# The scan's first two chunks started inside the projection's last steps, and the product of u with its sigmoid on VectorE

## The chip, the cores and the metric

The kernel runs on one NeuronCore of a Trainium2 chip. The metric is the time of one execution on the device in microseconds (us), as a median of several runs. The engines are named as in the profile: PE is TensorE's matmul, PEld its weight load, DVE is VectorE, ACT is ScalarE, POOL is GpSimd, and SP is the engine whose queue issues the DMAs. An engine executes its own program in order, and engines wait for one another on semaphores.

## The reference

Two layers over 8 images of 192 channels and 64x64 positions (L = 4096 positions), all in float32. Only the first layer is touched:

```python
xn = layernorm over channels of x
xz = einsum('dc,bchw->bdhw', in_proj_w, xn);  xc, z = split(xz, 2)
xc = silu(conv3x3_depthwise(xc) + conv_b)             # silu(u) = u * sigmoid(u)
xs = [xc, xc transposed, both reversed]               # 4 directions k
x_dbl = einsum('kcd,bkdl->bkcl', x_proj_w, xs);  dts, Bv, Cv = split(x_dbl, [12, 16])
dt = softplus(dt_proj_w @ dts + dt_proj_b)
h_t = exp(dt_t * A) * h_(t-1) + dt_t * B_t * u_t;  y_t = sum over n of h_t * C_t      # 4 states n
y = layernorm(sum of the 4 directions + Ds * xs) * silu(z);  x = x + out_proj_w @ y
```

The second layer is a non-local attention over the 4096 positions of each image (softmax of theta^T phi, then a weighted sum of g and a projection).

## The kernel before

One loop runs over the 8 images. In an image four stages follow one another: the projection (`run_project`), the scan (`run_chunks`), the mix (`run_mix`) and the attention (`run_attend`). Between two stages stands `barrier`: each engine drains, increments `stage_done`, and waits until all five have done so. No barrier stands inside a stage; there every engine has its own program of the same steps, ordered by hand, and semaphores with running counts link them.

**The projection** works on 8 chunks of 512 positions (`NCH` = 8, `T` = 512). `step(c, par, which)` does parts of four different chunks at once: with "n" it normalizes chunk c+1 (mean and variance by PE, `da`, `db`, `na`, `nb` on DVE), with "p" it projects chunk c (PE, L360 and L361) and makes `gate` = z * sigmoid(z), with "c" it convolves chunk c-2, and with "u" it finishes chunk c-3. The convolution of the first 128 channels is eight multiply-adds on DVE (L1039); that of the other 64 is six matmuls on PE (`remainder`, L371), which ACT takes from bank 5 into `u` (L694, semaphore `rem_free`). ACT then makes the sigmoid of u in the buffer `cs` by Exp, Ln and Exp (L681, L683, L685), and POOL multiplies `u` by `cs` in place (L937, semaphore `u_ready`). There is one buffer `cs`, so that the sigmoid of chunk w waits for the product of chunk w-1. Steps 3 to 6 are a loop that holds "npcu"; step 7 is "pcu", steps 8 and 9 are "cu", and step 10 is "u".

**The scan** walks 32 chunks (4 directions of 8). Counting from the scan's start as g, a chunk takes this path: PE's `xdbl` (L409, L410) projects u; ACT copies the result to `xd` (L729, `copy_xd`) and to `xhl` (L735, `copy_high`), and DVE takes the rest (`low_half`, L1084); SP saves rows of `xd` to memory and loads them back, broadcast to all partitions, into `bs` (L297 to L303); PE's `dtproj` (L417) makes the input of the softplus; ACT does five instructions on it (`soft_abs` to `soft_log`, L739 to L755), POOL adds one part to `dt` (`residue`, L945), DVE the other (`residue`, L1090, and `softplus`, L1096); POOL makes `du` = dt * u (`times_u`, L951) and `dbu` = B * du in three pieces (`drive`, L960); ACT makes the decays (L762), DVE scans (L1106) and multiplies by C (L1114), which PE spreads (`spread`, L428) and sums. DVE works on one chunk while the others prepare the next one or two. Ahead of the first chunk's scans stands a written-out head that prepares chunks 0 and 1.

The buffers of the scan (`xd`, `xhl`, `dt`, `bs`, `dbu`, `h` and others) lie over those of the projection (`xa`, `xb`, `na`, `nb`, `zs`, `cs` and others). Line numbers here and in the prediction are those of the kernel before.

## Time and profile before

| what | value |
|---|---|
| median of 3 runs | 9796.43 us (9791.25 to 9798.18) |
| the profiled execution, its own time | 9790.28 us |
| its span, first to last instruction | 9788.5 us |
| mean granted clock of PE over the span | 0.966 |
| busy: PE, DVE, ACT, POOL | 93%, 76%, 64%, 35% |
| chain of work that ended last: PE, issue, DVE, ACT, POOL | 68%, 13%, 13%, 3%, 2% |

An image takes about 1,220 us and all eight look alike. The profile has a page, with sums over the whole span, and views: busy time of the engines in chosen stretches, groups by line, and a timeline. In the timeline a row gives the start, the duration of the run of equal instructions, the engine and line, what is written from what, the count (x2), and in brackets how long the engine had been idle before it and who ended that. A float32 matmul of 512 columns shows as two records.

### The profile page before, as it was taken

Reading aid. Unit: us, or ns where it says so; the run is one execution under the profiler, and the core shown is the slowest. Engines: PE = TensorE matmul, PEld = TensorE weight load, DVE = VectorE, ACT = ScalarE, POOL = GpSimd, SP = SyncE. Lnnn points to the kernel's source line nnn. Section 1 sums busy time; section 2 is a strip of 40 time slices with the busy share of each in tenths; the row PEclk is TensorE's granted clock in tenths of the full one; section 3 lists DMA queues with packets and bytes.
Section 4 is the critical chain, followed back from the end, with each engine's and each line's share of the span. In section 5 each row is a group of like instructions: output and inputs, shape, how many; then the busy total and the mean of one; then the engine's idle time right before and its main releaser. Section 6 shows DMA issues by size and latency. Waiting matters only on the chain.

```text
span 9788.5 us, 105912 instructions
## 1 busy us (share of the span) xinstructions
PE 9055.4 (93%) x27076; PEld 4819.9 (49%) x27076; DVE 7434.1 (76%) x8241; ACT 6228.0 (64%) x7692; POOL 3449.1 (35%) x1937
## 2 busy tenths in 40 slices
PE   7999989999799998999979999899998999989999
PEld 3336733367333673336733367333663336633366
DVE  6987769876698766987669776697766977679776
ACT  5765667656676566765667556676566755667555
POOL 3850038500385003850038500485004850048500
PEclk9999989999899998999999999899999999989999
DMA  1320013200132001320013200132001320013200
GB/s 56 106 75 12 11 52 105 74 13 12 51 109 71 12 12 51 110 70 11 12 56 106 70 11 12 57 108 67 10 12 57 111 65 10 13 56 110 65 10 13
DMA packets 214540, 499.71 MB, mean 51 GB/s; under 512 B 71001, under 2 KB 71993, under 8 KB 181262
## 3 DMA queue, kind: packets, MB, share of 16 engines
q1 hardware_dynamic: 214030, 494.10, 16.5%
q8 instruction: 174, 2.85, 0.1%
q14 instruction: 336, 2.75, 0.1%
HBM read 466.39 MB, written 27.38 MB: 50 GB/s over the span
## 4 chain that ended last, share of the span: by engine, by line
PE 68%; issue 13%; DVE 13%; ACT 3%; POOL 2%; DVEq 1%; SPq 0%; ACTq 0%; POOLq 0%; DMA 0%
DVE h L1106 7%; PE ps L587 5%; PE ps L574 5%; PE ps L589 5%; PE ps L588 5%; PE ps L575 5%; PE ps L576 5%; PE ps L494 4%; PE ps L417 3%; PE ps L455 3%; PE ps L353 2%; PE ps L452 2%; PE ps L409 2%; PE ps L354 2%; PE ps L436 2%
## 5 line engine op out<-in xcount | busy, mean ns | idle before, releaser
L1232 DVE TENSOR_TENSOR pl<-pf,ph 128x1024 fp32r<-128x1024 f32 x1024 | 1254.4, 1225 | 1017.1 <-ACT ph L886 1008.9
L1106 DVE TENSOR_TENSOR_SCAN h<-ps,h,dbu 128x512 f32<-128x512 f32 x1536 | 1884.5, 1268 | 17.3 <-DVE h L1132 5.3
L960 POOL TENSOR_TENSOR dbu<-bs,du 128x1024 f32<-128x1024 f32 x768 | 1799.1, 2373 | 52.8 <-POOL du L951 52.8
L886 ACT ACTIVATE ph<-pf 128x1024 fp32r<-128x1024 f32 x1024 | 1085.7, 1060 | 762.8 <-PE ps L589 762.6
L906 POOL MEMSET sqb<- 64x512 f32 x16 | 8.3, 519 | 4002.3 <-issue 3997.4
L880 ACT ACTIVATE pf<-ps 128x1024 f32<-128x1024 f32 x1024 | 1050.0, 1025 | 531.4 <-PE ps L576 531.4
L762 ACT ACTIVATE ps<-dt,negA 128x512 f32<-128x512 f32 x1536 | 1033.3, 684 | 443.7 <-DVE h L1106 408.9
L1216 DVE TENSOR_REDUCE mx<-ps 128x1 f32<-128x512 f32 x1792 | 1168.6, 683 | 78.2 <-PE ps L494 59.6
L1114 DVE TENSOR_TENSOR hc<-h,ps 128x1024 f32<-128x1024 f32 x768 | 937.9, 1221 | 190.6 <-PE ps L428 107.3
L951 POOL TENSOR_TENSOR du<-dt,u 128x512 f32<-128x512 f32 x512 | 706.5, 1402 | 625.8 <-DVE dt L1096 625.8
L574 PE MATMUL ps<-thc,phh 97*128 97x512 f32 x2048 | 845.0, 413 | 6.7 <-ACT thc L863 6.7
L587 PE MATMUL ps<-ph,gth 128*97 128x512 f32 x2048 | 819.0, 400 | 11.7 <-DVE pl L1232 8.7
L575 PE MATMUL ps<-thc,phl 97*128 97x512 f32 x2048 | 814.2, 398 | 0.0
L576 PE MATMUL ps<-thc,phh 97*128 97x512 f32 x2048 | 811.7, 396 | 0.0
L589 PE MATMUL ps<-pl,gth 128*97 128x512 f32 x2048 | 810.2, 396 | 0.0
L428 PE MATMUL ps<-xhl,selr 128*128 128x512 f32 x1536 | 692.5, 532 | 126.6 <-DVE hc L1114 126.5
L588 PE MATMUL ps<-ph,gtl 128*97 128x512 f32 x2048 | 808.9, 395 | 0.0
L494 PE MATMUL ps<-phh,thc 96*128 96x512 f32 x1824 | 633.7, 408 | 47.3 <-POOLq L180 18.8
L945 POOL TENSOR_TENSOR dt<-dt,ze 128x1024 f32<-128x1024 f32 x256 | 605.4, 2365 | 101.5 <-ACT dt L755 101.5
L417 PE MATMUL ps<-xd,wdt 128*128 128x512 f32 x1024 | 520.2, 632 | 101.9 <-DVE dt L1096 94.8
L428 PEld LDWEIGHTS ps<-xhl,selr 128*128 128x128 f32 x1536 | 265.4, 190 | 589.9 <-DVE hc L1114 379.8
L1039 DVE SCALAR_TENSOR_TENSOR u<-pad,vecs,u 128x512 f32<-128x512 f32 (+1 forms) x512 | 491.0, 960 | 61.4 <-DVE db L1027 18.8
(188 smaller groups left out, 15586.0 us busy)
## 6 DMA issues: line engine op xcount, KB each, us to landing
bs<-rows SPq DMA_DIRECT2D x256, 1024.0 KB, 5.1
bs<-rows SPq DMA_DIRECT2D x512, 256.0 KB, 6.1
xa<-in_x SPq DMA_DIRECT2D x130, 256.0 KB, 2.9
xb<-in_x SPq DMA_DIRECT2D x130, 128.0 KB, 3.0
out<-fa SPq DMA_DIRECT2D x64, 256.0 KB, 2.0
rdb<-rden SPq DMA_DIRECT2D x56, 192.0 KB, 3.4
out<-fa SPq DMA_DIRECT2D x64, 128.0 KB, 2.3
rows<-xd SPq DMA_DIRECT2D x256, 8.0 KB
```

Of the source, the lines that this page charges most:

```text
L574: mm(dst, kk, thc[par][0][:, :], start=True, stop=False)
L575: mm(dst, phl[:, m * P:(m + 1) * P], thc[par][0][:, :], start=False, stop=False)
L576: q = mm(dst, kk, thc[par][1][:, :], start=False, stop=True)
L587: mm(dst, gth[:, m, :], ph[:, mp % 2, e, :], start=(m == 0), stop=False)
L588: mm(dst, gtl[:, m, :], ph[:, mp % 2, e, :], start=False, stop=False)
L589: q = mm(dst, gth[:, m, :], pl[:, mp % 2, e, :], start=False, stop=(m == MT - 1))
L880: A(pf[:, mp % 2, :, :], ps[:, 2 * (mp % 2):2 * (mp % 2) + 2, :], ACT.Exp)\
L886: A(ph[:, mp % 2, :, :], pf[:, mp % 2, :, :], ACT.Copy).then_inc(S["ph_ready"], 1)
L960: pool.tensor_tensor(dbu[:, q, :, :], bs[par][:, q, :, :], du[:, r:r + 1, :].to_broadcast([P, 2, T]), ALU.mult).then_inc(S["dbu_ready"], 1)
L1106: dve.tensor_tensor_scan(h[:, j, ::step], ps[:, 2 + e, ::step], dbu[:, q, e, ::step], h[:, j, end:end + 1], ALU.mult, ALU.add)\
L1216: dve.tensor_reduce(mx[:, t, m:m + 1], ps[:, 5 + j % 2, :], AX.X, ALU.max)\
L1232: TT(pl[:, mp % 2, :, :], pf[:, mp % 2, :, :], ph[:, mp % 2, :, :].bitcast(F32), ALU.subtract)\
```

## The change

The barrier between the projection and the scan is removed, and the remaining three are renumbered. Of the head of the scan, pieces are moved between the projection's steps 8, 9 and 10, by a function `early(n)` that `run_project` calls ahead of step 8 + n. What the barrier guarded is guarded by waits on single semaphores. The product of `u` with `cs` goes from POOL to DVE, at the end of a step. The clearing of `xd` and `xhl` on DVE goes to the image's start, and that of `h` stays ahead of the first scan.

```diff
         def run_project(eng, step, early=None):
             ...
             step(NCH - 1, 1, "pcu")
-            step(NCH, 0, "cu")
-            step(NCH + 1, 1, "cu")
-            step(NCH + 2, 0, "u")
+            for n, which in ((0, "cu"), (1, "cu"), (2, "u")):
+                if early:
+                    early(n)
+                step(NCH + n, n % 2, which)
# SP
-                barrier(sp, b, 0)
+                sp.wait_ge(S["xc_ready"], b * NCH + NCH)
+                sp.sem_inc(mark, 1)
# PE
-                xdbl(0, 0, g_0)
-                dtproj(0, g_0)
+                def early(n):
+                    if n == 0:
+                        pe.wait_ge(S["u_ready"], b * NCH + 2)
+                        pe.sem_inc(mark, 1)
+                        xdbl(0, 0, g_0)
+                        dtproj(0, g_0)
+                    elif n == 1:
+                        pe.wait_ge(S["u_ready"], b * NCH + 3)
+                        pe.sem_inc(mark, 1)
+                        xdbl(0, 1, g_0 + 1)
+                run_project(pe, step, early)
+                dtproj(0, g_0 + 1)
+                pe.wait_ge(S["gate_ready"], b * NCH + (NCH + 1))
+                pe.wait_ge(S["rem_free"], b * NCH + (NCH + 1))
+                pe.sem_inc(mark, 1)
                 spread(0, 0, g_0)
-                xdbl(0, 1, g_0 + 1)
-                dtproj(0, g_0 + 1)
+                pe.wait_ge(S["u_ready"], b * NCH + (NCH + 1))
                 run_chunks(pe, b, body)
# ACT
-                copy_xd(g_0)
-                copy_high(0, g_0)
-                soft_abs(g_0)
-                soft_relu(g_0)
-                soft_exp(g_0)
-                soft_one(g_0)
-                soft_log(0, g_0)
-                copy_xd(g_0 + 1)
+                def early(n):
+                    if n == 0:
+                        act.wait_ge(S["scan_set"], b + 1)
+                        copy_xd(g_0)
+                        copy_high(0, g_0)
+                    elif n == 1:
+                        soft_abs(g_0)
+                        soft_relu(g_0)
+                        soft_exp(g_0)
+                        soft_one(g_0)
+                        soft_log(0, g_0)
+                    else:
+                        copy_xd(g_0 + 1)
+                        copy_high(1, g_0 + 1)
+                run_project(act, step, early)
+                act.wait_ge(S["gate_ready"], b * NCH + (NCH + 1))
+                act.sem_inc(mark, 1)
                 decay(0, 0, 0, g_0 * NP, 0, g_0)
                 decay(0, 0, 1, g_0 * NP, 0, g_0)
                 soft_abs(g_0 + 1)
                 soft_relu(g_0 + 1)
                 soft_exp(g_0 + 1)
-                copy_high(1, g_0 + 1)
                 soft_one(g_0 + 1)
                 soft_log(1, g_0 + 1)
# POOL
-                def step(c, par, which):
-                    if "u" in which:
-                        ...
-                        pool.tensor_tensor(u[:, :, sl], u[:, :, sl], cs[:, :, :], ALU.mult).then_inc(S["u_ready"], 1)
                 residue(0, g_0)
+                pool.wait_ge(S["u_ready"], b * NCH + 2)
                 times_u(0, 0, 0, g_0)
-                for q in range(NP):
-                    drive(q, g_0 * NP + q, 0, g_0)
+                pool.wait_ge(S["xc_ready"], b * NCH + NCH)
+                pool.sem_inc(mark, 1)
+                drive(0, g_0 * NP, 0, g_0)
+                drive(1, g_0 * NP + 1, 0, g_0)
+                residue(1, g_0 + 1)
+                drive(2, g_0 * NP + 2, 0, g_0)
+                pool.wait_ge(S["u_ready"], b * NCH + (NCH + 1))
# DVE, end of step(c, par, which)
+                    if "u" in which:
+                        w = b * NCH + (c - 3)
+                        dve.wait_ge(S["cs_ready"], w * 3 + 3)
+                        sl = bass.ds((c - 3) * T, T)
+                        TT(u[:, :, sl], u[:, :, sl], cs[:, :, :], ALU.mult).then_inc(S["u_ready"], 1)
# DVE, body of the scan: the second residue goes behind the first scans
                         if q == 0 and nxt:
-
+                            if not before:
+                                residue(g + 1)
                             softplus(1 - par, g + 1)
# DVE, head of the scan
-                low_half(0, g_0)
-                residue(g_0)
-                softplus(0, g_0)
-                low_half(1, g_0 + 1)
-                residue(g_0 + 1)
+                def early(n):
+                    if n == 1:
+                        low_half(0, g_0)
+                    elif n == 2:
+                        residue(g_0)
+                        softplus(0, g_0)
+                        low_half(1, g_0 + 1)
+                run_project(dve, step, early)
+                dve.wait_ge(S["u_ready"], b * NCH + (NCH + 1))
+                dve.wait_ge(S["rem_ready"], b * NCH + NCH)
+                dve.sem_inc(mark, 1)
+                dve.memset(h[:, :, T - 1:T], 0.0).then_inc(S["zero_h"], 1)
+                dve.wait_ge(S["zero_h"], b * (K + 3) + 4)
+                dve.sem_inc(mark, 1)
```

The order of DVE's instructions around the border of the two stages. Before, the last multiply-add of chunk 7 is followed by the barrier (L181), three clearings, and the whole head of the scan:

```order
L1039 SCALAR_TENSOR_TENSOR u<-pad,vecs,u 128x512
L181 ISA
L1075 MEMSET xd 128x512
L1076 MEMSET h 128x6
L1078 MEMSET xhl 64x512 x2
L1079 ISA
L1083 ISA
L1084 TENSOR_TENSOR xhl<-ps,xhl 32x512
L1089 ISA
L1090 SCALAR_TENSOR_TENSOR ps<-ps,za 128x1024
L1096 SCALAR_TENSOR_TENSOR dt<-ps,dt 128x1024
L1083 REGISTER_ALU
```

In the changed kernel (its own line numbers: L1052 is the multiply-add, L1087 the product with `cs`, L1096 `low_half`, L1102 `residue`, L1108 `softplus`) the same place on DVE reads:

```order
L1052 SCALAR_TENSOR_TENSOR u<-pad,vecs,u 128x512
L1085 ISA
L1087 TENSOR_TENSOR u<-u,cs 128x2x512
L1101 ISA
L1102 SCALAR_TENSOR_TENSOR ps<-ps,za 128x1024
L1108 SCALAR_TENSOR_TENSOR dt<-ps,dt 128x1024
L1095 REGISTER_ALU
L1096 TENSOR_TENSOR xhl<-ps,xhl 32x512
L1087 TENSOR_TENSOR u<-u,cs 128x2x512
L1161 MEMSET h 128x6
```

The first L1087 is the product of chunk 6, the second that of chunk 7; the softplus of chunk 0 and `low_half` of chunk 1 now stand between them. The same border on ACT, before: the last two chunks' copies and sigmoids (L694 to L685), the barrier (L181), then the first copy of the scan:

```order
L694 ACTIVATE u<-ps,vecs 128x512
L700 REGISTER_ALU
L681 ACTIVATE cs<-u 128x1024
L683 ACTIVATE cs<-cs 128x1024
L685 ACTIVATE cs<-cs 128x1024
L181 ISA
L723 REGISTER_ALU
L726 ISA
L728 ISA
L729 ACTIVATE xd<-ps 20x512
```

In the changed kernel ACT has, from the softplus of chunk 0 on (L745 to L761), the copy and sigmoid of chunk 6 (L706, L693 to L697) and the copies of the scan's chunk 1 (L735, L741):

```order
L756 ACTIVATE ps<-za 128x1024
L760 REGISTER_ALU
L761 ACTIVATE dt<-za 128x1024
L706 ACTIVATE u<-ps,vecs 128x512
L693 ACTIVATE cs<-u 128x1024
L694 ISA
L695 ACTIVATE cs<-cs 128x1024
L696 REGISTER_ALU
L697 ACTIVATE cs<-cs 128x1024
L734 ISA
L735 ACTIVATE xd<-ps 20x512
L740 ISA
```

The five softplus instructions of chunk 0 stand ahead of the sigmoid of chunk 6, and `copy_xd` of chunk 1 stands ahead of that of chunk 7.

## Rows read from the trace of the kernel before

**Rows 1.** Busy time by stretch; after POOL the granted clock, DMA share and GB/s

```profile
105.35:119.08 13.73, 13.73 (x33) 6.06 (x32) 11.49 (x15) 11.47 (x16) 2.63 (x1) 1.00 0.00 0
133.90:166.10 32.20, 21.34 (x48) 8.85 (x49) 25.13 (x27) 20.43 (x23) 10.22 (x4) 0.91 0.00 0
166.10:192.50 26.40, 14.81 (x20) 5.63 (x21) 6.53 (x9) 12.97 (x16) 11.39 (x6) 0.63 0.38 121
207.70:222.50 14.80, 13.04 (x31) 5.28 (x30) 13.94 (x13) 11.60 (x17) 11.33 (x6) 1.00 0.34 107
```

**Rows 2.** Timeline of TensorE (PE) in the projection's loop: start, duration, line, count

```profile
119.08 1.02 PE L353 MATMUL ps<-xa,avg 128*128 128x512 f32 x2
...
127.67 5.31 PE L371 MATMUL ps<-pad,tapw 128*128 x12
```

**Rows 3.** Timeline of VectorE (DVE) in the projection's loop

```profile
121.00 0.69 DVE L1026 TENSOR_TENSOR da<-xa,ps 128x512 f32<-128x512 f32 x1 [0.60 <-PE ps L354]
...
122.73 2.54 DVE L1039 SCALAR_TENSOR_TENSOR u<-pad,vecs,u  x3 [0.45 <-DVE db L1027]
...
127.24 4.41 DVE L1039 SCALAR_TENSOR_TENSOR u<-pad,vecs,u  x3 [0.16 <-DVE u L1039]
131.57 0.68 DVE L1063 TENSOR_TENSOR na<-da,rstd 128x512 f32<-128x512 f32 x1
...
133.37 0.67 DVE L1068 TENSOR_TENSOR gate<-ps,zs 64x512 f32 x1
```

**Rows 4.** The convolution's line on VectorE: minimum, median, maximum in ns

```profile
L1039 DVE SCALAR_TENSOR_TENSOR u<-pad,vecs,u x512: 733/752/2743, 65.5 to 8699.6; - x86, 128x512 f32<-128x512 f32 x85
```

**Rows 5.** The page's group of a VectorE product with both inputs in SBUF

```profile
L1232 DVE TENSOR_TENSOR pl<-pf,ph 128x1024 fp32r<-128x1024 f32 x1024 | 1254.4, 1225 | 1017.1 <-ACT ph L886 1008.9
```

**Rows 6.** Timeline of all engines, the projection's last steps

```profile
139.35 5.31 PE L371 MATMUL ps<-pad,tapw 128*128 128x512 f32 x12
...
142.75 0.78 ACT L717 ACTIVATE u<-ps,vecs 128x512 f32<-128x512 f32 x1
...
144.70 0.69 ACT L694 ACTIVATE u<-ps,vecs 128x512 f32<-128x512 f32 x1 [1.17 <-PE ps L371]
145.47 1.06 ACT L681 ACTIVATE cs<-u 128x1024 f32<-128x1024 f32 x1
...
163.41 2.34 POOL L937 TENSOR_TENSOR u<-u,cs 128x1024 f32<-128x1024 f32 x1 [5.60 <-ACT cs L685]
```

**Rows 7.** Timeline of all engines, the scan's head

```profile
166.10 2.07 PE L409 MATMUL ps<-u,wx 128*128 128x512 f32 x2 [8.92 <-POOLq L180]
...
166.78 1.03 DVE L1078 MEMSET xhl<- 64x512 f32 x2 [0.17 <-issue]
...
170.00 0.59 ACT L729 ACTIVATE xd<-ps 20x512 f32<-20x512 f32 x1 [6.66 <-PE ps L410]
...
174.36 1.02 ACT L739 ACTIVATE za<-ps 128x1024 f32<-128x1024 f32 x1 [3.30 <-PE ps L417]
...
179.35 2.34 POOL L945 TENSOR_TENSOR dt<-dt,ze 128x1024 f32<-128x1024 f32 x1 [13.60 <-ACT dt L755]
...
181.80 1.23 DVE L1096 SCALAR_TENSOR_TENSOR dt<-ps,dt 128x1024 f32<-128x1024 f32 x1 [2.23 <-POOL dt L945]
...
183.19 2.49 POOL L951 TENSOR_TENSOR du<-dt,u 128x512 f32<-128x512 f32 x2 [1.51 <-DVE dt L1096]
...
185.93 6.96 POOL L960 TENSOR_TENSOR dbu<-bs,du 128x1024 f32<-128x1024 f32 x3 [0.25 <-POOL du L951]
```

**Rows 8.** Timeline of VectorE, the scans of the first two chunks

```profile
192.52 2.46 DVE L1106 TENSOR_TENSOR_SCAN h<-ps,h,dbu 128x512 f32<-128x512 f32 x2
...
207.72 2.46 DVE L1106 TENSOR_TENSOR_SCAN h<-ps,h,dbu 128x512 f32<-128x512 f32 x2
```

**Rows 9.** Busy time and granted clock of a stretch without matmuls

```profile
160.00:162.00 2.00, 0.00 (x0) 0.00 (x0) 0.00 (x0) 1.86 (x2) 0.00 (x0) 0.61 0.00 0
```

**Rows 10.** The page's DMA issues: the line of the broadcast loads

```profile
bs<-rows SPq DMA_DIRECT2D x512, 256.0 KB, 6.1
```

More of the change, by code:

```diff
@@ L174, in build @@
         mark = sem("mark")
-        stages = 4
+        stages = 3
         def barrier(eng, b, n):
@@ L225, in run_chunks, with run_project @@
                     body(k, n % 2, b * G + (k * NCH + n), place(k, n - 1), place(k, n), place(k, n + 1), place(k, n + 2))
-        def run_project(eng, step):
+        def run_project(eng, step, early=None):
             step(-1, 1, "n")
@@ L304, in _ @@
                 run_chunks(sp, b, body)
-                barrier(sp, b, 1)
+                barrier(sp, b, 0)
                 with sp.Fori(0, NCH // 2) as cc:
@@ L308, in _ @@
                         load(b, (b * 2 + 1) * NCH + cc * 2 + q, cc * 2 + q, q)
-                barrier(sp, b, 2)
+                barrier(sp, b, 1)
                 for q in range(2):
@@ L337, in _ @@
                 store(NCH - 1)
-                barrier(sp, b, 3)
+                barrier(sp, b, 2)
             sp.wait_ge(S["out_stored"], nb * (32 * NCH) + 32)
@@ L400, in step @@
                         remainder(c - 2)
-                run_project(pe, step)
-                barrier(pe, b, 0)
                 def xdbl(k, c, g):
@@ L546, in _ @@
                 run_mix(pe, step)
-                barrier(pe, b, 2)
+                barrier(pe, b, 1)
                 def theta(c, i, before):
@@ L650, in _ @@
                 output(last, 1)
-                barrier(pe, b, 3)
+                barrier(pe, b, 2)
         @block.scalar
@@ L718, in step @@
                           scale=vecs[:, V_TAP + 4:V_TAP + 5]).then_inc(S["tap_ready"], 1)
-                run_project(act, step)
-                barrier(act, b, 0)
-                act.wait_ge(S["scan_set"], b + 1)
                 def copy_xd(g):
@@ L813, in _ @@
                 add_y1(K - 1, 0, g_0 + G - 1)
-                barrier(act, b, 1)
+                barrier(act, b, 0)
                 def split_theta(i, par):
@@ L855, in _ @@
                 run_mix(act, step)
-                barrier(act, b, 2)
+                barrier(act, b, 1)
                 def take_shift(i, par):
@@ L890, in _ @@
                 read_sum(i_0 + (NCH - 1))
-                barrier(act, b, 3)
+                barrier(act, b, 2)
         @block.gpsimd
@@ L929, in _ @@
                                                None, ALU.mult).then_inc(S["tapw_ready"], 1)
-                def step(c, par, which):
-                    if "u" in which:
-                        w = b * NCH + (c - 3)
-                        pool.wait_ge(S["cs_ready"], w * 3 + 3)
-                        sl = bass.ds((c - 3) * T, T)
-                        pool.tensor_tensor(u[:, :, sl], u[:, :, sl], cs[:, :, :], ALU.mult).then_inc(S["u_ready"], 1)
-                run_project(pool, step)
-                barrier(pool, b, 0)
                 def residue(par, g):
@@ L964, in body @@
                     if nxt:
-                        residue(1 - par, g + 1)
+                        if before:
+                            residue(1 - par, g + 1)
                         times_u(*nxt, 1 - par, g + 1)
@@ L986, in _ @@
                     pool.sem_inc(mark, 1)
+                barrier(pool, b, 1)
                 barrier(pool, b, 2)
-                barrier(pool, b, 3)
         @block.vector
@@ L1069, in step @@
                             .then_inc(S["gate_ready"], 1)
-                run_project(dve, step)
-                barrier(dve, b, 0)
+                    if "u" in which:
[3 more added lines that the diff above has]
+                        TT(u[:, :, sl], u[:, :, sl], cs[:, :, :], ALU.mult).then_inc(S["u_ready"], 1)
                 dve.memset(xd[:, :], 1.0).then_inc(S["zero_h"], 1)
-                dve.memset(h[:, :, T - 1:T], 0.0).then_inc(S["zero_h"], 1)
                 for t in xhl:
                     dve.memset(t[R:P, :].bitcast(F32), 0.0).then_inc(S["zero_h"], 1)
-                dve.wait_ge(S["zero_h"], b * (K + 3) + 4)
+                dve.wait_ge(S["zero_h"], b * (K + 3) + 3)
                 dve.sem_inc(S["scan_set"], 1)
@@ L1209, in _ @@
                 run_mix(dve, step)
-                barrier(dve, b, 2)
+                barrier(dve, b, 1)
                 def top(j, i):
@@ L1296, in _ @@
                 finish(NCH - 1, last, 1)
-                barrier(dve, b, 3)
+                barrier(dve, b, 2)
 def kernel(x, L0_conv_ln_w, L0_conv_ln_b, L0_conv_in_proj_w, L0_conv_conv_w, L0_conv_conv_b, L0_conv_x_proj_w,
```

6 lines of the change are left out of this document (3 added, 3 removed).

## The prediction, made before the changed kernel ran

> **What bounds the kernel now.** I read the stages first. In the projection's loop the busy view shows one step of 13.73 us in which PE is busy for all of it, at the full clock, and DVE for 11.49 [rows 1]. The timeline agrees: the mean of the next chunk starts 13.73 us after the last one, and the step ends with twelve records of `remainder` (5.31 us) [rows 2]. In the scan DVE is the bound: busy 13.94 of 14.80 us, PE 13.04 [rows 1]. Between these two lies the border that the change touches: from the loop's end (133.9) to the barrier PE is busy for 21.34 of 32.20 us, and in the next 26.40 us, the scan's head, DVE for 6.53, ACT for 12.97 and PE for 14.81, at a mean clock of 0.63 [rows 1]. There no engine is the bound. It is a chain of single steps, and that is what a reader should see in the rows of the head: nearly each has some microseconds of idle time in its bracket [rows 7]. The border costs as much in each of the eight images.
>
> The figure to follow is the start of the scans of the scan's chunk 1, at 207.72, since from there on DVE works in its steady rhythm; chunk 0's begin at 192.52 [rows 8].
>
> **The product on DVE, in the loop.** It adds eight instructions per image. The same shape with both inputs in SBUF takes 1.225 us on DVE while POOL is idle [rows 5]. It also takes POOL's product away, and that gives DVE something back. The convolution's instruction takes 0.752 us in the median, but up to 2.743 [rows 4], and the run of three at 127.24 took 4.41 us against 2.54 for the run at 122.73 [rows 3]: 1.87 us more, in the stretch in which POOL's product ran. So DVE's sum per step is -1.87 + 1.22 = -0.65 us. The Trainium skill ("SBUF — State Buffer", who interferes with whom) gives the mechanism: a VectorE instruction with two SBUF inputs and a GpSimd instruction that reads SBUF exclude each other, the later one waiting for the whole of the earlier. By that rule the trace agrees.
>
> Is the loop faster for it? The product stands behind `gate` and ahead of the next `da`. Without the stretch the convolution ends at 129.7 in place of 131.57; `na` then waits for ACT's `rstd` until about 130.95, so that `gate` ends at 133.4 in place of 134.04 [rows 3] and the product at 134.65. The next `da` is due at 121.00 + 13.73 = 134.73, when PE's mean is ready (its row had waited 0.60 us for PE). It is not late. Nor is it earlier, because PE has no idle time. I cost the loop at nothing; the cover is PE, and without it a step would take DVE's own 12.4 us, a gain of 1.3. The clearings (two of `xhl` 1.03 us [rows 7], that of `xd` about half as much) go to the image's start, ahead of DVE's first work, which waits there for PE's first mean. I cost them at nothing too, or 1.5 us per image if that cover is gone.
>
> **The border, step by step.** I use the first image's clock. The waits that come last decide each line.
>
> 1. ACT ends step 7 at 143.6, as now (142.75 + 0.78) [rows 6]. PE ends `remainder` of chunk 5 some 0.6 us sooner than 139.35 + 5.31 = 144.66, because `gate` is sooner: 144.0.
> 2. New: PE does `xdbl` of the scan's chunk 0 (four records at 0.43 us, the full-clock rate of rows 2, to 145.8), and ACT, in order, waits for it, then does two copies (0.6 and 0.5), to 147.0. Behind that wait ACT's copy of chunk 5 and its sigmoid are queued, 0.7 + 3.2 us (L694 to the end of L685; three at 1.06 [rows 6]): 150.9, where it was 148.7. PE does `dtproj` to 148.4 and `remainder` of chunk 6 to 153.7.
> 3. ACT's five softplus instructions, from 174.36 until POOL takes over at 179.35 [rows 7], 4.9 us,, end at 155.8; copy and sigmoid of chunk 6 at 159.6; two copies at 160.7. PE ends `xdbl` of chunk 1 at 155.5, and `remainder` of chunk 7, which waits for ACT's copy, at 161.7.
> 4. ACT's copy and sigmoid of chunk 7: 165.8, now 163.34. So u is complete 2 us later than now (165.75, the end of POOL's last product [rows 6]). That is the price of interleaving.
> 5. DVE: product 5 at 152.1, `low_half` 0.7, convolution of chunk 7 to 159.1; POOL's `residue` of chunk 0 falls in it, from 155.8, which costs the 1.87 us: 160.9. Product 6 to 162.15, `residue` and `softplus` of chunk 0 at 1.23 each: 164.5. That softplus ends now at 181.80 + 1.23 = 183.03 [rows 7]: 18.5 us later.
> 6. POOL: `du` 2.5 us (183.19 [rows 7]) to 167.1; then its first `drive` (6.96 / 3 = 2.3 us) and DVE's product 7 want the same stretch, and the first scan starts at about 170.2 where it is 192.52: between 169.6, if they don't meet, and 170.8.
> 7. Chunk 0: scans and product with C 3.7 us (173.9), then on DVE the moved `residue` 1.2, and `softplus` of chunk 1, which waits for POOL's `residue`, itself behind two `drive`s: 176.7. ACT's five for chunk 1 end at 172, in time. Then 2 x 3.7 + 0.7 + 1.2 us: 186.1.
>
> Against 207.72 that is 21.6 us. SP's DMAs are moved too: rows of chunk 0 are saved from 146.5 on and loaded back 6.1 us after issue [rows 10], long before `drive` at 167; those of chunk 1 from 160 on, for a `drive` at 180; SP has nothing else queued.
>
> From this I take two deductions. PE's clock reads 0.61 in the stretch 160 to 162, after PE's last matmul at 166.10 - 8.92 = 157.2 [rows 7, 9]. In my schedule PE has no such pause until 170, when it waits 3.8 us for the first hc; `dtproj` of chunk 2 might then run at half clock, 3.7 for 1.7 us, and make the last `spread` and product of chunk 0 up to 1.5 us late. Half of it: 0.6. And some 20 handovers that I counted too short: 0.5. That makes **20.5 us per image, 164 us for eight**. The sum is made against the profiled execution's own 9790.28 us (span 9788.5 and 1.8 around it): 9626. The median of the runs lies 6.15 us above the profiled one, so that I predict **9632 us**.
>
> The likeliest case's own range: a sum of single steps that misses by 3 to 4 us per image, 9605 to 9665.
>
> **The rivals.**
>
> *The loop gains too* (0.10). If DVE and not PE closed the loop, each of some six steps would give up to 1.3 us: 62 us more, 9570. PEld's wait for `gate` speaks for it; PE's 13.73 of 13.73 against it.
>
> *POOL and DVE get in each other's way at the border* (0.13). Product 7 comes at 165.8, amid `du` and three `drive`s. If it lost to two `drive`s and the last convolutions to more than one POOL instruction, 2.3 + 2.3 us and, through chunk 1's `softplus`, as much as 5 us per image would be lost: 9672. The Trainium skill, on the page named above, speaks for this: the later instruction "fully blocks" until the first finishes. By that rule alone, with product 7 behind one `drive`, the sum would be 8 x 2.3 = 18 us worse, 9650.
>
> *The clock* (0.05). If PE, with pauses of 1 to 3 us, fell to half at step 8, the two `remainder`s (5.3 us each) and `xdbl` and `dtproj` of both chunks would take about 15 us more in the chain: 5.5 us gained per image, 9752. Against it: the clock fell only 3 to 4 us into a complete standstill (since 166.10 - 8.92 = 157.2 [rows 7, 9]).
>
> *It doesn't do what it says* (0.03). ACT is one queue; what is begun early there delays the rest. My step 4 puts this at 2.5 us. Only if it came near 20 would nothing be left: 9796.
>
> *Slower* (0.04). The scan's first chunks now start after a thin stretch of PE. If PE came into them at half clock and stayed there, its 13.04 us of work per chunk would become up to 22 to 26 against DVE's 14.8: 8 us lost per chunk. From the third such chunk on the change loses; with four, 8 x (32 - 20.5) = 92 us: 9888. Against it: the clock is back at 1.00 in the stretch of chunk 1 now, after a head with a clock of 0.63 [rows 1].
>
> **How the numbers follow.** Forecast 0.65, the rivals as above. The range that leaves no more than 2 in 10 outside takes in the likeliest case and the meeting of POOL and DVE up to a loss of 7 us per image, and below, a per-image gain of 25: 9594 to 9690. Faster by over 0.2% (20 us, about what a measurement of this kernel can tell from no change) are the first four cases: 0.93; same 0.03; slower 0.04.
>
> **What would show it.** In the changed profile, first image: a step of the loop still 13.73 us, with no multiply-add over 0.8 us in it; the product's row at 1.22 us; the last product of u at 167 to 168; first scan near 170; chunk 1's scans near 186 to 187; DVE's busy time up by about 64 x 1.22 less 64 x 1.9, that is down some 40 us, POOL's down by 64 x 2.6 = 166 us; clock above 0.9 from 134 to 170. I am wrong if ACT's sigmoid of chunk 7 comes after 170, if the clock falls there, or if the loop's step changes.

## The result, and the profile after

The changed kernel takes 9647.41 us (median of 4 runs, 9642.17 to 9653.10) against 9793.84 for the kernel before on the same occasions (9782.22 to 9798.18): 146 us less, a ratio of 0.9852 with the interval 0.9839 to 0.9864. In a second comparison it took 9642.80 us, ratio 0.9844 (0.9830 to 0.9858). One of the 15 runs of the kernel before in that comparison took 14447.48 us, at a mean granted clock of 0.563, and stands outside the ratios. The prediction was 9632 us, range 9594 to 9690.

Line numbers from here on are those of the kernel in question. In the changed one L1052 is the convolution's multiply-add on DVE, L1087 the product of u with `cs`, L1102 `residue`, L1108 `softplus`, L1118 the scan, L1126 the product with C; on POOL L951 is `residue`, L957 `du` and L966 `drive`; on PE L373 is `remainder` and L416 `dtproj`.

From the page of the changed kernel, the busy times:

```profile
PE 9020.4 (93%) x27076; PEld 4814.2 (50%) x27076; DVE 7422.2 (77%) x8305; ACT 6225.7 (65%) x7692; POOL 3292.1 (34%) x1873
```

Busy times fell little: PE by 35 us, DVE by 12, POOL by 157 (against 3449.1). The span fell by 137 in this execution. What left is idle time.

The groups of DVE that hold the convolution and the product, with busy time, mean ns and idle time:

```profile
L1052 DVE SCALAR_TENSOR_TENSOR u<-pad,vecs,u 128x512 f32<-128x512 f32 (+1 forms) x512 | 400.5, 782 | 61.1 <-DVE db L1040 18.8 <-DVE u L1052 10.4
...
L1087 DVE TENSOR_TENSOR u<-u,cs 128x1024 f32 (+1 forms) x64 | 79.7, 1246 | 11.7 <-ACT cs L697 11.7
```

The convolution's 512 instructions take 400.5 us, where they took 491.0: 90.5 less, that is 48 stretches of 1.9 us (a stretch is an instruction that takes up to 2.74 in place of 0.75 us). The product costs 79.7. I had written 64 stretches. There were seven per image (POOL's last product met no convolution), and one is left, under POOL's `residue`. So DVE's busy time fell by 12 us and not by some 40.

The last step of the projection's loop on DVE in the changed kernel:

```profile
119.73 0.69 DVE L1039 TENSOR_TENSOR da<-xa,ps 128x512 f32<-128x512 f32 x1 [0.17 <-PE ps L356]
...
125.97 2.54 DVE L1052 SCALAR_TENSOR_TENSOR u<-pad,vecs,u  x3 [0.16 <-DVE u L1052]
129.68 0.69 DVE L1076 TENSOR_TENSOR na<-da,rstd 128x512 f32<-128x512 f32 x1 [1.16 <-ACT rstd L689]
...
131.49 0.67 DVE L1081 TENSOR_TENSOR gate<-ps,zs 64x512 f32 x1
132.09 1.21 DVE L1087 TENSOR_TENSOR u<-u,cs 128x1024 f32 x1
```

These answer to [rows 3]. The three multiply-adds at 125.97 take 2.54 us, no longer 4.41. DVE uses what it has got back for waiting: 1.16 us for ACT's `rstd`. The product follows `gate`. This `da` comes 13.73 us after the one before it (at 106.00), as in the kernel before: the convolution, 1.9 us shorter, has bought nothing in the loop, and the product has cost nothing.

The border on DVE in the changed kernel, first image:

```profile
151.62 8.24 DVE L1052 SCALAR_TENSOR_TENSOR u<-pad,vecs,u 128x512 f32<-128x512 f32 x8
159.78 1.22 DVE L1087 TENSOR_TENSOR u<-u,cs 128x1024 f32<-128x1024 f32 x1
...
162.29 1.22 DVE L1108 SCALAR_TENSOR_TENSOR dt<-ps,dt 128x1024 f32<-128x1024 f32 x1
...
164.55 1.48 DVE L1087 TENSOR_TENSOR u<-u,cs 128x1024 f32<-128x1024 f32 x1 [0.32 <-ACT cs L697]
...
170.06 2.46 DVE L1118 TENSOR_TENSOR_SCAN h<-ps,h,dbu 128x512 f32<-128x512 f32 x2 [3.74 <-POOL dbu L966]
...
186.65 2.46 DVE L1118 TENSOR_TENSOR_SCAN h<-ps,h,dbu 128x512 f32<-128x512 f32 x2
```

Chunk 0's scans begin at 170.06, chunk 1's at 186.65, where [rows 8] have 192.52 and 207.72. (The first image's loop runs 1.27 us ahead of that of [rows 3] in this execution, 119.73 for 121.00, so that this much of the difference is no gain of the border.) The 8.24 at 151.62 are eight multiply-adds of which one is stretched; the last product of u, at 164.55, takes 1.48 in place of 1.21 us; and before the first scan DVE waits 3.74 us for POOL's `drive`. POOL and PE at the same place:

```profile
154.50 2.44 POOL L951 TENSOR_TENSOR dt<-dt,ze 128x1024 f32<-128x1024 f32 x1 [117.62 <-ACT dt L761]
163.68 3.48 POOL L957 TENSOR_TENSOR du<-dt,u 128x512 f32<-128x512 f32 x2 [6.74 <-DVE dt L1108]
167.56 4.67 POOL L966 TENSOR_TENSOR dbu<-bs,du 128x1024 f32<-128x1024 f32 x2 [0.40 <-POOL du L957]
```

```profile
155.14 5.39 PE L373 MATMUL ps<-pad,tapw 128*128 128x512 f32 x12 [0.99 <-ACT u L706]
163.66 3.75 PE L416 MATMUL ps<-xd,wdt 128*128 128x512 f32 x4 [3.13 <-DVE dt L1108]
...
176.41 3.72 PE L416 MATMUL ps<-xd,wdt 128*128 128x512 f32 x4 [1.28 <-DVE dt L1108]
```

POOL's `du` takes 3.48 us, where the pair takes 2.49 in [rows 7]: the last product of u stands in its way. PE's pauses are as short as forecast up to 161. Then it waits 3.13 us for DVE's `softplus`; the granted clock reads 0.86 in 160 to 164 and 0.50 in 164 to 168, and `dtproj` runs at half rate, 3.75 and 3.72 us, against 1.98 for the first one. The first scan is not later for it: it comes 50.3 us behind `da` in all eight images.

The second image shows what the first one doesn't. First the kernel before, then the changed one, each with the last `da` of the projection and the scans of chunks 0 and 1 on DVE:

```profile
1343.05 0.69 DVE L1026 TENSOR_TENSOR da<-xa,ps 128x512 f32<-128x512 f32 x1 [0.59 <-PE ps L354]
```

```profile
1412.88 2.46 DVE L1106 TENSOR_TENSOR_SCAN h<-ps,h,dbu 128x512 f32<-128x512 f32 x2
...
1427.42 2.46 DVE L1106 TENSOR_TENSOR_SCAN h<-ps,h,dbu 128x512 f32<-128x512 f32 x2
```

```profile
1322.06 0.69 DVE L1039 TENSOR_TENSOR da<-xa,ps 128x512 f32<-128x512 f32 x1 [0.17 <-PE ps L356]
```

```profile
1372.39 2.46 DVE L1118 TENSOR_TENSOR_SCAN h<-ps,h,dbu 128x512 f32<-128x512 f32 x2 [3.74 <-POOL dbu L966]
...
1384.16 1.28 DVE L1118 TENSOR_TENSOR_SCAN h<-ps,h,dbu 128x512 f32<-128x512 f32 x1 [0.67 <-ACT ps L768]
1386.97 1.22 DVE L1126 TENSOR_TENSOR hc<-h,ps 128x1024 f32<-128x1024 f32 x1 [1.52 <-PE ps L427]
...
1390.20 1.28 DVE L1118 TENSOR_TENSOR_SCAN h<-ps,h,dbu 128x512 f32<-128x512 f32 x1
```

From `da` to the scans of chunk 1 the second image took 84.37 us before and takes 68.14 now: 16.2 us less, while the first one went from 86.72 (207.72 - 121.00) to 66.92, 19.8 less. Read from the same three starts in all eight images, the means are:

| kernel, profiled execution | `da` to first scan | chunk 0 | sum | times 8, against before |
|---|---|---|---|---|
| before | 70.48 | 15.15 | 85.63 | |
| changed | 50.33 | 17.44 | 67.77 | -143 |
| changed, second comparison | 50.33 | 17.12 | 67.45 | -145 |

So the border carries the change. Each of the other parts of an image (the rest of the scan, the mix, the attention, the projection up to `da`) differs by less than 0.6 us.

### The profile page after: what moved, and what is told of

The parts are those of the page before. It is cut to its first block and busy times, and to the rows that moved or that the text cites. A ratio compares the mean times of both kernels' runs of the same rounds, so it can differ in the third digit from the quotient of the medians.

```text
span 9651.3 us, 105800 instructions
## 1 busy us (share of the span) xinstructions
PE 9020.4 (93%) x27076; PEld 4814.2 (50%) x27076; DVE 7422.2 (77%) x8305; ACT 6225.7 (65%) x7692; POOL 3292.1 (34%) x1873
## 3 DMA queue, kind: packets, MB, share of 16 engines
q1 hardware_dynamic: 214030, 494.10, 16.8%
## 5 line engine op out<-in xcount | busy, mean ns | idle before, releaser
L1118 DVE TENSOR_TENSOR_SCAN h<-ps,h,dbu 128x512 f32<-128x512 f32 x1536 | 1884.2, 1267 | 50.3 <-POOL dbu L966 32.6
L966 POOL TENSOR_TENSOR dbu<-bs,du 128x1024 f32<-128x1024 f32 x768 | 1799.2, 2372 | 54.1 <-POOL du L957 54.1
L1126 DVE TENSOR_TENSOR hc<-h,ps 128x1024 f32<-128x1024 f32 x768 | 937.4, 1221 | 198.4 <-PE ps L427 118.5
L957 POOL TENSOR_TENSOR du<-dt,u 128x512 f32<-128x512 f32 x512 | 715.0, 1419 | 647.6 <-DVE dt L1108 646.9
L951 POOL TENSOR_TENSOR dt<-dt,ze 128x1024 f32<-128x1024 f32 x256 | 605.9, 2367 | 922.4 <-ACT dt L761 922.4
L416 PE MATMUL ps<-xd,wdt 128*128 128x512 f32 x1024 | 509.2, 621 | 81.8 <-DVE dt L1108 74.7
L454 PE MATMUL ps<-hc,foldw 128*128 128x512 f32 x1024 | 495.1, 606 | 0.0
```

Source lines behind the costliest of these rows:

```text
L966: pool.tensor_tensor(dbu[:, q, :, :], bs[par][:, q, :, :], du[:, r:r + 1, :].to_broadcast([P, 2, T]), ALU.mult).then_inc(S["dbu_ready"], 1)
L1118: dve.tensor_tensor_scan(h[:, j, ::step], ps[:, 2 + e, ::step], dbu[:, q, e, ::step], h[:, j, end:end + 1], ALU.mult, ALU.add)\
L1126: TT(hc[:, q, :, :], h[:, 2 * q:2 * q + 2, :], ps[:, 4:6, :], ALU.mult).then_inc(S["hc_ready"], 1)
```

## The experiments

Every kernel was timed in turn with the kernel before, whose medians on these occasions were 9789.12 to 9794.99 us; a difference of a few us between two rows is therefore to be read in the last column as well. That column is the mean over eight images of the stretch from the last `da` of the projection to the scans of chunk 1, read as above.

| run | what | median us | ratio, interval | border us |
|---|---|---|---|---|
| changed, second comparison | | 9642.80 | 0.9844 (0.9830 to 0.9858) | 67.45 |
| e1 | the product on DVE alone | 9760.95 | 0.9963 (0.9949 to 0.9977) | 81.95 |
| e2 | the overlap, product on POOL | 9661.03 | 0.9865 (0.9849 to 0.9881) | 69.62 |
| e3 | no barrier, nothing interleaved | 9719.23 | 0.9922 (0.9905 to 0.9939) | 76.23 |
| e4 | changed, PE's waits in chunk 0 filled | 9634.47 | 0.9838 (0.9821 to 0.9854) | 65.97 |
| e4, again | | 9634.65 | 0.9836 (0.9822 to 0.9850) | 65.98 |
| e5 | changed, `du` of chunk 0 on DVE | 9638.52 | 0.9842 (0.9826 to 0.9859) | 66.56 |
| e6 | e4 and e5 | 9639.79 | 0.9842 (0.9825 to 0.9858) | 66.96 |
| e7 | changed, each product twice | 9700.80 | 0.9903 (0.9886 to 0.9919) | 71.22 |
| e8 | e6, `residue` of chunk 0 on DVE | 9636.23 | 0.9841 (0.9824 to 0.9857) | 66.53 |
| e9 | before, PE's waits in the head filled | 9795.57 | 1.0001 (0.9992 to 1.0010) | 85.42 |

### The parts: e1, e2, e3

e1 is the kernel before with one edit:

```diff
# POOL: no product, and so no part in the projection
-                        pool.tensor_tensor(u[:, :, sl], u[:, :, sl], cs[:, :, :], ALU.mult).then_inc(S["u_ready"], 1)
-                run_project(pool, step)
# DVE, end of step
+                        TT(u[:, :, sl], u[:, :, sl], cs[:, :, :], ALU.mult).then_inc(S["u_ready"], 1)
```

> The product of u moved to VectorE, barrier and head of the scan as before. Theory (PE covers the loop; the chain at the border holds the gain): a loop step stays 13.73 us, the convolutions of the last steps lose their 1.9 us stretches and the last product takes 1.2 in place of 2.3 us, so that the barrier comes about 3 us sooner per image: 9794 - 26 = 9768 us. Rival A (freeing VectorE from POOL's product is what pays): most of the 146 us, below 9700 us. Rival B (the product costs VectorE time): slower than before by up to 8 x 8 x 1.2 = 78 us.

34 us less, where the theory has 26; both rivals fell. Of the 8 us too much, 5 are the clock: the head's first `dtproj` ran at half rate in three of eight images of the kernel before and in none of e1, a mean of 0.65 us per image. The convolution's line in e1 (minimum, median, maximum in ns), and DVE's last product:

```profile
L1032 DVE SCALAR_TENSOR_TENSOR u<-pad,vecs,u x512: 736/752/754, 66.5 to 8674.1; - x86, 128x512 f32<-128x512 f32 x85
```

```profile
162.60 1.23 DVE L1067 TENSOR_TENSOR u<-u,cs 128x1024 f32<-128x1024 f32 x1 [3.36 <-ACT cs L685]
```

With no POOL instruction left in the projection's steps, none of 512 multiply-adds takes over 754 ns, while 2743 was the maximum in [rows 4]. That shows that POOL's instruction makes the stretch. The gain lies at the border: 3.7 us per image. u is complete 2.95 us sooner (41.80 for 44.75 us behind `da`), by a convolution no longer stretched and by a last product of 1.23 in place of 2.34 us; the rest is that clock.

e2 is the changed kernel with POOL's `step` put back, its `residue` of chunk 0 standing between products 6 and 7:

> The whole overlap of the two stages, the product left on POOL. Theory: the first scan comes later than in the changed kernel by the longer last product (2.3 for 1.2 us), by one or two stretched convolutions (1.9 us each) and by POOL's du waiting behind it, some 4 us per image: 9647 + 32 = about 9680 us. Rival (the moved product is the main part): above 9740 us. Rival (the product's place does not matter): 9647 us.

It lost 14 to 18 us to the changed kernel's two medians, not 32: the overlap gives nearly all without the product. The first scan comes 2.8 us later (53.13 for 50.33 us behind `da`), and chunk 0 is 0.6 to 0.9 us shorter. DVE, then POOL, in e2:

```profile
148.42 8.25 DVE L1063 SCALAR_TENSOR_TENSOR u<-pad,vecs,u 128x512 f32<-128x512 f32 x8
...
162.83 1.23 DVE L1114 SCALAR_TENSOR_TENSOR dt<-ps,dt 128x1024 f32<-128x1024 f32 x1 [4.90 <-POOL dt L951]
...
171.98 2.46 DVE L1124 TENSOR_TENSOR_SCAN h<-ps,h,dbu 128x512 f32<-128x512 f32 x2 [5.07 <-POOL dbu L966]
```

```profile
158.08 2.35 POOL L983 TENSOR_TENSOR u<-u,cs 128x1024 f32<-128x1024 f32 x1 [5.89 <-ACT cs L697]
160.38 2.35 POOL L951 TENSOR_TENSOR dt<-dt,ze 128x1024 f32<-128x1024 f32 x1
```

DVE, freed of three products, is early, and waits 4.90 us for POOL's `residue`, which stands behind the 2.35 us product. `softplus` ends at 164.1, 45.2 us after this kernel's `da` at 118.84, against 43.8 in the changed one. The two edits don't add: 34 us alone, 14 to 18 on top of the overlap. What both would have saved, they save once; which wait it was isn't taken apart here.

e3 is the changed kernel with one edit on each of PE, ACT and DVE:

```diff
-                run_project(pe, step, early)
+                run_project(pe, step)
+                for n in range(3):
+                    early(n)
```

> No barrier and the product on VectorE, but the early pieces stand behind the projection's last step in place of between steps 8, 9 and 10. Theory (both parts count: starting without the barrier, and interleaving): TensorE begins the head at 157, but ScalarE's five softplus instructions begin only behind its last sigmoid, near 164 in place of 149.5, so that the first scan comes at about 177 in place of 170: 9647 + 8 x 7 = 9703 us. Rival (the barrier alone was the cost, interleaving gives back what it takes): 9647 us or less. Rival (removing the barrier is worth nothing, the chain is the same): about 9768 us, as the product alone.

It lost 72 to 76 us to the changed kernel, where the theory has 56. In six of its eight images the first `dtproj` ran slower than the full rate (3.78 us in five, 2.45 in one), in the changed kernel in none; that is about 1.2 us per image of the difference. The first scan on DVE in e3 (its `da` stands at 119.63):

```profile
178.72 2.46 DVE L1122 TENSOR_TENSOR_SCAN h<-ps,h,dbu 128x512 f32<-128x512 f32 x2 [4.70 <-POOL dbu L970]
```

The first scan is 59.1 us behind `da` here and 58.5 in the mean, 50.3 in the changed kernel. So the ladder is: the product 34 us, removing the barrier another 42 (9760.95 to 9719.23), moving pieces between the steps another 72 or more. The border column says the same: 3.7, 5.7 and 8.5 to 8.8 us per image.

The middle step is not the barrier alone, since e3 keeps the new order in the head, above all on DVE, where `residue` of chunk 1 now stands behind the first scans. In e1, as in the kernel before, the first scan starts 4.2 us after POOL's first `drive` has ended (66.83 and 62.58 us behind `da`), held up by that `residue`; in e3 it follows the `drive` at once (58.48 and 58.35), and chunk 0 is 2.6 us longer (17.75 for 15.12). What is common to both orders is `softplus` of chunk 0: it ends 4.4 us sooner in e3 (52.93 for 57.33). No run removes the barrier and nothing else, so that the 5.7 us are those of the barrier, the moved clearings and this order together.

### The clock in chunk 0: e4 and e9

The third image in the changed kernel, busy times of PE, PEld, DVE, ACT and POOL and then the granted clock:

```profile
2573.00:2577.00 4.00, 2.25 (x6) 0.68 (x4) 0.29 (x2) 3.97 (x5) 3.60 (x2) 1.00 0.14 31
2577.00:2581.00 4.00, 0.00 (x0) 0.00 (x0) 3.63 (x4) 2.63 (x4) 4.00 (x3) 0.82 0.00 0
2581.00:2585.00 4.00, 2.62 (x4) 1.34 (x5) 3.96 (x5) 0.33 (x1) 3.92 (x3) 0.50 0.01 2
```

PE had 2.25 us of work in 2573 to 2577 and none in the next 4 us; the clock fell from full (2.4 GHz) to half (1.2). `dtproj` came next at half rate, and what hangs on it came late: in the rows above, of the second image, the scan at 1384.16 waits 0.67 us for ACT's decay, which stood behind the first softplus instruction on that `dtproj`, and chunk 0's last product with C, at 1386.97, waits 1.52 us for `spread`. In the first and the eighth image the clock fell earlier, and chunk 0 is shorter (16.59 and 16.51 us against 17.6 to 17.8). e4 gives PE something to do there, in chunk 0 of each image only:

```diff
+                def fill(n):
+                    for _ in range(n):
+                        mm(ps[:, 1, :], eye[:, :], u[:, 0, 0:T], start=True, stop=True)
...
                     if before:
                         sum_rest(*before, g - 1)
+                    else:
+                        fill(5)
                     spread(1, par, g)
+                    if not before:
+                        fill(1)
```

> The changed kernel with six float32 matmuls into the unused bank 1 while TensorE waits in the first chunk of each image's scan (five ahead of the second spread, one behind it). They are extra work and change no output. Theory (chunk 0 takes 17.4 us in the mean because TensorE's clock falls to 0.50 in its wait and the next projection of dt runs at half rate): the clock stays at 1.00, chunk 0 takes about 15.8 us, 9647 - 8 x 1.6 = 9634 us. Rival (chunk 0 is bound by VectorE and POOL, whose instructions are the same): 9647 us. Rival (the fill delays the spreads): slower by up to 8 x 2 us.

9634.47, and 9634.65 in the second comparison, 8 us below the changed kernel there, where 13 were expected. The same image in e4:

```profile
2570.00:2574.00 4.00, 3.52 (x9) 1.25 (x7) 2.73 (x3) 3.19 (x5) 4.00 (x3) 1.00 0.00 0
2574.00:2578.00 4.00, 2.10 (x5) 0.98 (x6) 3.96 (x4) 0.33 (x1) 3.96 (x2) 1.00 0.00 0
2578.00:2582.00 4.00, 4.00 (x11) 1.84 (x10) 3.88 (x4) 3.20 (x5) 3.79 (x3) 1.00 0.42 168
```

The clock stays at 1.00 here, the `dtproj` in chunk 0 takes 1.95 us in all eight images, and chunk 0 takes 15.64 us in every one. The time followed the clock, with VectorE's and POOL's work unchanged, so that the rival of these two as the bound fell. The medians differ by 8 to 13 us; the intervals of the two ratios to the kernel before overlap, but on one chip all five runs of e4 (9632.08 to 9636.06) lie below all five of the changed kernel (9640.51 to 9644.12).

e9 asks how much of the 146 us could have been had with the clock alone: the kernel before with `fill(7)` ahead of the second `dtproj` and `fill(4)` behind it.

> The kernel before, with the barrier and the product as they were, and float32 matmuls into the unused bank 1 in TensorE's two waits of the scan's head (seven ahead of the second dtproj, four behind it). Theory (most of the gain of the change is work begun sooner, the clock is a small part): the second dtproj runs at the full clock, 1.9 us sooner, and chunk 0 takes 14.4 us: 2.6 us per image, 9790 - 21 = 9770 us. Rival (the slow clock of the head, 0.63, was what the head cost): a large part of the 146 us, 9700 us or less.

Nothing was had: ratio 1.0001 (0.9992 to 1.0010). PE, POOL, then DVE, in e9:

```profile
183.89 1.96 PE L417 MATMUL ps<-xd,wdt 128*128 128x512 f32 x4 [0.66 <-DVE dt L1102]
...
197.43 3.75 PE L417 MATMUL ps<-xd,wdt 128*128 128x512 f32 x4 [0.91 <-DVE dt L1102]
```

```profile
193.57 2.38 POOL L951 TENSOR_TENSOR dt<-dt,ze 128x1024 f32<-128x1024 f32 x1
```

```profile
196.06 1.22 DVE L1102 SCALAR_TENSOR_TENSOR dt<-ps,dt 128x1024 f32<-128x1024 f32 x1 [0.82 <-POOL dt L951]
```

The second `dtproj` runs at the full rate, 1.96 for 3.7 us, and the first scan is 2.0 us sooner after `da` in the mean. But POOL's work has not moved: its `residue` of chunk 1 stands behind three `drive`s that hang on `softplus` of chunk 0, and starts at 193.57, 71.9 us behind `da` (121.69 in this execution), where it started 71.8 us behind it before. DVE, sooner at its `softplus`, waits for it (0.82 us), the clock has fallen again at 197.43, and chunk 0 takes 16.97 in place of 15.15 us. So with POOL's work where it is, the clock in the head costs the head 2.0 us and the kernel nothing. The rival fell, and so did my own 20 us. What a fill in chunk 0 as well would have given the kernel before was not run; in its image with the fastest chunk 0 (`dtproj` there at 1.95 us) chunk 0 took 14.37 us, which makes 6 us for eight images, as an estimate from that row.

### The room on DVE: e7

```diff
+                        TT(yt[:, :, :], u[:, :, sl], cs[:, :, :], ALU.mult)
                         TT(u[:, :, sl], u[:, :, sl], cs[:, :, :], ALU.mult).then_inc(S["u_ready"], 1)
```

> The changed kernel with each product of u and its sigmoid done twice on VectorE (first into a buffer that nobody reads): 1.2 us more VectorE work per step, no other change. Theory (TensorE closes the projection's loop and VectorE has 1.3 us of room per step): the loop's step stays 13.73 us; only at the border, where VectorE is in the chain, some 3 us per image are lost: 9647 + 24 = 9671 us. Rival (VectorE is as much the bound as TensorE, the added product was just paid by the stretches that left): every step longer by 1.2 us, 9647 + 77 = 9724 us.

9700.80: 53 to 58 us more, between the 24 of the theory and the 77 of the rival. One step of e7's loop in the busy view, and on DVE:

```profile
119.65:134.27 14.62, 13.24 (x31) 5.39 (x29) 11.96 (x17) 11.48 (x16) 0.00 (x0) 1.00 0.00 0
```

```profile
118.65 0.69 DVE L1076 TENSOR_TENSOR na<-da,rstd 128x512 f32<-128x512 f32 x1 [1.04 <-ACT rstd L689]
...
121.06 1.21 DVE L1087 TENSOR_TENSOR yt<-u,cs 128x1024 f32<-128x1024 f32 x1
122.20 1.21 DVE L1088 TENSOR_TENSOR u<-u,cs 128x1024 f32 x1
123.33 0.67 DVE L1039 TENSOR_TENSOR da<-xa,ps 128x512 f32<-128x512 f32 x1
...
133.27 0.69 DVE L1076 TENSOR_TENSOR na<-da,rstd 128x512 f32<-128x512 f32 x1 [1.16 <-ACT rstd L689]
```

The step has grown from 13.73 to 14.62 us (118.65 to 133.27), and no engine is busy all through it: PE 13.24, DVE 11.96, ACT 11.48. (In the two steps ahead of it PE was still busy throughout, as it caught up; DVE's steps took 14.6 us there too.) What closes the step is a ring over two engines. `da` is late behind the second product; ACT can begin its squares and both sigmoids only then and gives `rstd` some 9.9 us later, for which DVE waits 1.16 us (`na` at 133.27, `da` at 123.33); then `na`, `nb`, `gate` and the products lead to the next `da`. In the changed kernel this ring is 9.95 + 2.4 + 1.2 us and leaves 0.17 us of wait for PE, the bracket on `da` at 119.73. Added work of 1.13 us per step lengthened it by 0.89. So the product is free in the loop, but with 0.2 us to spare.

### POOL and DVE at the border: e5, e6, e8

e5 makes the two products `dt * u` of chunk 0 on DVE, behind its `softplus`, and POOL waits for `du_ready`; e6 adds the fill of e4; e8 also puts POOL's `residue` of chunk 0 on DVE.

> The changed kernel with the product dt * u of each image's first scan chunk on VectorE (two of 0.6 us) in place of POOL (3.5 us there, with the last product of u in its way). Theory (VectorE products and POOL instructions exclude each other): POOL's first drive starts near 165 and holds back VectorE's product 7 until 167.3; first scan at 168.6 in place of 170.1: 9647 - 8 x 1.4 = 9636 us. Rival (they do not exclude each other, the stretch had another cause): first scan at 167.5, 9627 us. Rival (the last softplus, not the first scan, sets chunk 1): 9647 us.

> The fill of TensorE's waits and the product dt * u on VectorE together. Theory (two separate waits of one chain, both on the way to chunk 1): their gains add, 9634 - 8 x 1.4 = 9623 us. Rival (with the clock at 1.00 chunk 0 is bound by POOL's three drives and its residue): 9634 us.

> As the last, and POOL's residue of the first chunk (2.4 us, which stretches the convolution by 1.9) on VectorE too (1.2 us, behind product 6). Theory: VectorE loses 1.2 us and gets 1.9 back, softplus of chunk 0 comes 0.7 us sooner: 9623 - 6 = 9617 us. Rival (TensorE's remainder of chunk 7 and ScalarE's sigmoid set the end of the border, not VectorE): 9623 us.

e5 came 4 to 9 us below the changed kernel's two medians, where 11 were expected. The product and POOL's `drive` exclude each other in either order, by which starts first. In the first image the product does (1.22 us, at 167.37), and POOL's two `drive`s take 5.72 us, 4.67 in the changed kernel:

```profile
167.39 5.72 POOL L966 TENSOR_TENSOR dbu<-bs,du 128x1024 f32<-128x1024 f32 x2 [8.76 <-DVE du L1158]
```

In the seven others `drive` starts first, by some 0.02 us, as the theory has it. The product then takes 3.4 us and the second `drive` waits for it in turn. The second image, DVE, POOL and PE:

```profile
1369.22 3.42 DVE L1086 TENSOR_TENSOR u<-u,cs 128x1024 f32<-128x1024 f32 x1
```

```profile
1369.20 5.65 POOL L966 TENSOR_TENSOR dbu<-bs,du 128x1024 f32<-128x1024 f32 x2 [8.72 <-DVE du L1158]
```

```profile
1372.77 2.07 PE L408 MATMUL ps<-u,wx 128*128 128x512 f32 x2 [3.16 <-DVE u L1086]
```

So the first scan comes only 0.4 us sooner (49.9 us behind `da`), and PE's `xdbl` of chunk 2, which needs all of u, starts 49.5 us behind `da`, where it starts at 46.4 in most images of the changed kernel.

e6 was slower than e4 by 5 us, so that the gains don't add, and the rows show why. In the seven images with the late `xdbl`, the useless matmuls of the fill stand behind it in PE's queue and push back what follows: `dtproj` of chunk 2 starts 58.4 to 60.0 us behind `da`, in e5 55.9 to 56.5. PE in the second image of e6:

```profile
1372.80 2.07 PE L408 MATMUL ps<-u,wx 128*128 128x512 f32 x2 [3.15 <-DVE u L1094]
...
1376.20 4.46 PE L459 MATMUL ps<-u,eye 128*128 128x512 f32 x10
1380.10 1.03 PE L427 MATMUL ps<-xhl,selr 128*128 128x512 f32 x2
...
1381.82 1.88 PE L416 MATMUL ps<-xd,wdt 128*128 128x512 f32 x4
```

That is the rival which e4 had (the fill delays the spreads), and it holds here. The rival of e6 itself, POOL's `residue` as the next bound, shows in the first image alone, where DVE's `softplus` waits 0.70 us for it. e8, at 9636.23, is not to be told from e6 or e4, and its first image confirms the reading: there the product started first, and chunk 0 took 15.64 us, as in e4; in the seven others the product took 3.4 us and chunk 0 16.8 to 17.3. A fill with fewer matmuls beside e5 was not run. The best version measured is e4.

## Why the prediction was right, step by step

**The mechanism held.** The loop's step is unchanged, the clearings at the start cost nothing seen. In the prediction's clock (1.27 us on top of the changed kernel's first image), the last product of u ends at 167.3, forecast 167.0, and `softplus` of chunk 0 at 164.8, forecast 164.5. The waits of the forecast are those of the trace up to the first scan. In chunk 0 one of them is not there: DVE's `softplus` of chunk 1 did not wait for POOL's `residue`.

**Signs that came out otherwise.** DVE's busy time fell by 12 us and not by 40, since 48 stretches left and not 64. The scans of chunk 1 came at 187.9 in the prediction's clock, not near 186 to 187. And "I am wrong if the clock falls there" was met in the first image: the mean from 134 to 170 is 0.91, but it reads 0.50 from 164 on. "In my schedule PE has no such pause until 170" is the step that missed it. By that very schedule PE ends `remainder` at 161.7 and its next work, `dtproj` of chunk 1, waits for `softplus`, which ends at 164.5; the trace has 3.13 us of wait there. It did no harm, since the first scan hangs on POOL and comes at 50.3 us in every image.

**Sizes that were off.** Predicted 164 us, measured 146 (150 in the second comparison). In four terms, per image:

1. *One image was taken for eight.* "The border costs as much in each of the eight images" is wrong: 86.72 us is the first image's border, and 85.63 the mean, 84.2 to 86.8 in all. The difference is mostly the clock: the first `dtproj` of the head ran at half rate, 3.7 to 3.8 us, in three of the eight images, the first among them, and at full rate, 1.98, in the others. That took 1.1 us from the gain.
2. *The clock in chunk 0*, costed at 0.6 us, costs 1.5 to 1.8: 17.12 and 17.44 us against e4's 15.64. That is 0.9 to 1.2 too little.
3. *POOL and DVE in each other's way*, costed at half a `drive` at most by the choice of 170.2: the first scan came 50.33 us behind `da`, that is at 171.3 in the prediction's clock, 1.1 later. The product stood in POOL's `du` (3.48 for 2.49 us). The rule of the Trainium skill ("SBUF — State Buffer", who interferes with whom) speaks of this, and e1, e5 and the `du` row agree with it; its price in the prediction, 2.3 us, was twice what the place cost.
4. On the other side stand 0.5 us that I had deducted for handovers, and chunk 0 of 15.6 us without the clock's share, 0.3 less than the 15.9 written.

With the second comparison's 17.12 us for chunk 0, 1.1 + 0.9 + 1.1 less 0.8 are 2.3 us, against 20.5 - 18.2 = 2.3 measured at the border (85.63 - 67.45); with the first one's 17.44 they are 2.6, against 20.5 - 17.9. That three errors one way were partly made up by a fourth is luck, and so is part of the nearness of 9632: the gain was put 9 to 12% too high. (The lower end of the range, a gain of 25 us per image, would be 9596 and not 9594.)

**A step that failed without harm.** "I cost the loop at nothing; the cover is PE, and without it a step would take DVE's own 12.4 us, a gain of 1.3." The cost of nothing was right, the reason incomplete. I had added up DVE alone and left out that its `na` waits for ACT, which waits for DVE's `db`. The ring over both closes at 13.5 us, so that the room was 0.2 us and not 1.3; the 12.4 have no working in the prediction, and DVE's busy time in a step of the changed kernel is 10.9 us. e7 measured the ring.

**The rivals.** No gain in the loop (13.73 us stays). The meeting of POOL and DVE took 1.1 us, not 5. The clock did not fall at step 8; it fell before 164 in the first image and in chunk 0 in most others, and was back by chunk 1. ACT's sigmoid of chunk 7 ended 2.5 us later than before, at 165.8 in the prediction's clock as step 4 had it, and u was complete 1.5 us later, where the prediction wrote 2; e3 shows what that bought, 8.5 us.

**What stays open.** In kernels with the product on DVE the stretch from chunk 1 to the end of the first direction takes 101.0 us, in those with it on POOL 101.4, with the same instructions in it. And from the first to the last of DVE's products `pl` the attention took 439.55 us per image in this execution of the changed kernel and 439.30 before. The runs don't tell why.

## What to carry to other kernels

Ask of a barrier between two stages what stands behind it: taking it away, with the order of the head that this allowed, was worth 5.7 us per image, and setting the pieces of the head behind it, one chain with every engine half idle, between steps that left those engines room, another 8.5. To cost an added instruction, close the ring over all engines and not the sum of one: PE was busy for 13.73 of 13.73 us in the kernel before, and with the product on DVE the ring through DVE and ACT stood 0.2 us behind it. Before a saving is multiplied by the number of repetitions, read it in the others as well, above all where the clock may be at either level. The same goes for an explanation: what e5 and e6 show in the first image is not what happens in the other seven.

## What the runs showed of the hardware that I had not expected

- The float32 multiply-add on VectorE with both tensors in SBUF takes 0.75 us alone and up to 2.74 while GpSimd reads SBUF, and never more than 0.754 in e1, where GpSimd does nothing beside it. The blocking goes both ways: a VectorE product made GpSimd's `du` 3.48 us for 2.49, and two `drive`s 5.72 for 4.67. A start 0.02 us sooner or later decides who waits: in e5 the same product took 1.22 us in one image and 3.4 in seven. Scans (1.25 to 1.29 us, all 1536) and products with one input in PSUM (1.22 us, all 768) ran beside GpSimd without it.
- Useless matmuls can pay: six per image, in waits of TensorE of up to 5.76 us, kept `dtproj` at the full rate (1.95 for up to 3.75 us) and took 8 us or more off the kernel. Eleven per image in the head of the kernel before paid nothing, since POOL's work stood behind the wait that was shortened; and in e6, where the wait had moved, they stood in the way of what followed.
